# Gate, up and context weights turned by the host, and the four-chunk Hadamard mix moved from the weights to the inputs, in a two-layer gated kernel on one core

## The reference, cut to what matters

```
x = x + tanh(g_xattn[0]) * moe0(layernorm(x), tokens, ctx, ctx, ctx)      # expert by token id, 4 experts
x = x + tanh(g_ffn[0])   * hadamard_ffn(layernorm(x))
x = x + tanh(g_xattn[1]) * wkv(w, u, layernorm(x), ctx)                    # a scan over time, values = ctx
x = x + tanh(g_ffn[1])   * moe1(layernorm(x))                              # shared expert + top 2 of 8
```

```
g = silu(einsum('bsd,fd->bsf', h, Wg[e]));  u = einsum('bsd,fd->bsf', h, Wu[e])
y = einsum('bsf,df->bsd', g * u, Wd[e])
```

```
x      = fwht(x * SU_ug) / 64
x_up   = x @ W_up.T   * (Wscale_ug[:2048] * 64)
x_gate = x @ W_gate.T * (Wscale_ug[2048:] * 64)
x      = fwht(silu(x_gate) * x_up * SU_dp) / 64
x      = x @ W_down.T * (Wscale_dp * 64)
```

## Time and profile before

| | |
|---|---|
| median of 3 runs | 1342.69 us (1342.31 to 1342.88) |
| the profiled execution's own time | 1343.7 us |
| its span | 1342.0 us |
| instructions | 18348 |
| PE busy | 1256.9 us (94%) |
| DVE, ACT, POOL busy | 656.1, 446.4, 407.3 us |
| mean granted TensorE clock | 0.973 |

### The profile page before, as it was taken

How to read it: one execution, slowest core, us unless ns; L and a number is a source line. 1 busy time by engine, 2 the same in 40 slices (tenths; PEclk the granted TensorE clock), 3 DMA queues, 4 the chain that set the end, 5 groups by cost and what they waited for, 6 DMA issues and landing times.

```text
span 1342.0 us, 18348 instructions
## 1 busy us (share of the span) xinstructions
PE 1256.9 (94%) x6226; PEld 1062.6 (79%) x6227; DVE 656.1 (49%) x1104; ACT 446.4 (33%) x755; POOL 407.3 (30%) x333
## 2 busy tenths in 40 slices
PE   4999989999999999999999998999999999999960
PEld 3788878878888888888888877888788888888850
DVE  6555257544365655755456457766232232223216
ACT  3333342233234433343244346552222222222210
POOL 2221112000013211221234224247866240017854
PEclk9899999999999999999999999988999999999995
DMA  6822267553658875784866421045636242224457
GB/s 204 274 79 64 83 232 266 185 222 135 251 196 310 291 287 185 282 323 170 267 254 219 159 73 54 28 159 213 213 121 188 78 161 78 74 73 156 142 161 254
DMA packets 88395, 240.42 MB, mean 179 GB/s; under 512 B 8300, under 2 KB 35144, under 8 KB 76040
## 3 DMA queue, kind: packets, MB, share of 16 engines
q1 hardware_dynamic: 64824, 160.19, 33.1%
q0 software_dynamic: 23040, 79.08, 18.3%
q10 hardware_dynamic: 464, 0.27, 0.1%
HBM read 163.75 MB, written 75.76 MB: 178 GB/s over the span
## 4 chain that ended last, share of the span: by engine, by line
PE 87%; DVE 5%; DMA 2%; POOL 2%; issue 2%; ACT 1%; POOLq 0%; ACTq 0%; DVEq 0%
PE bank L1176 26%; PE bank L1346 19%; PE bank L1204 13%; PE bank L1384 10%; PE bank L1101 4%; PE bank L1121 4%; PE bank L1313 2%; PE bank L1131 2%; PE bank L1364 1%; POOL fin_low L784 1%; PE bank L1148 1%; DVE xres L1937 1%; DVE wl L1523 1%; PE bank L1087 1%; DMA yg<-y_sorted,slot 1%
## 5 line engine op out<-in xcount | busy, mean ns | idle before, releaser
L1176 PE MATMUL bank<-xTh,G 128*128 128x512 f32 x1024 | 278.6, 397 | 1.8 <-DVE xTl L1629 1.8
L1176 PEld LDWEIGHTS bank<-xTh,G 128*128 128x128 f32 x1024 | 188.8, 188 | 42.5 <-issue 3.4
L1346 PE MATMUL bank<-W,dxh 128*128 (+2 forms) x880 | 205.8, 376 | 8.4 <-DVE dmid L1783 5.1
L1346 PEld LDWEIGHTS bank<-W,dxh 128*128 128x128 f32 x880 | 164.2, 191 | 23.8 <-issue 8.5
L1204 PE MATMUL bank<-DN,bhh 128*128 128x512 f32 x512 | 158.0, 390 | 0.0
L1176 PE MATMUL bank<-xTl,G 128*128 128x512 f32 x512 | 137.4, 390 | 0.0
L1384 PE MATMUL bank<-W,dhh 112*128 (+1 forms) x440 | 126.1, 408 | 1.8 <-ACT dys L994 1.8
L1651 DVE SCALAR_TENSOR_TENSOR bs<-bank,tab,bs 128x512 f32<-128x512 f32 x64 | 47.5, 742 | 161.1 <-PE bank L1176 161.1
L1783 DVE TENSOR_TENSOR dmid<-bank,dsg 128x448 f32<-128x448 f32 x55 | 34.2, 622 | 173.9 <-ACT dsg L984 173.9
L1204 PEld LDWEIGHTS bank<-DN,bhh 128*128 128x128 f32 x512 | 96.2, 188 | 21.3 <-issue 1.7
L1176 PEld LDWEIGHTS bank<-xTl,G 128*128 128x128 f32 x512 | 96.1, 188 | 20.7
(11 more groups left out here) (250 smaller groups left out, 1989.6 us busy)
## 6 DMA issues: line engine op xcount, KB each, us to landing
G<-gate_up_split SPq DMA_DIRECT2D x48, 1024.0 KB, 7.0
DN<-down_split SPq DMA_DIRECT2D x24, 1024.0 KB, 4.9
wst<-in_L_ffn_w POOLq DMA_DIRECT2D x24, 896.0 KB, 5.9
gate_up_split<-G SPq DMA_DIRECT2D x16, 1024.0 KB, 7.3
y_all<-dys SPq DMA_DIRECT2D x55, 256.0 KB, 2.0
xs_sorted<-zero POOLq DMA_DIRECT2D x3, 3328.0 KB, 20.7
xsd<-xs_sorted SPq DMA_DIRECT2D x39, 256.0 KB, 3.0
down_split<-DN SPq DMA_DIRECT2D x8, 1024.0 KB, 3.9
```

The source lines that it names most:

```text
L1176: mm = pe.matmul(bank[m][:, :], G[:, c % 2, f, h, m, i, :], a[b % 2][:, i, :], start=(n == 0), stop=(n == 3 * DC - 1))
L1346: mm = pe.matmul(bank[o][:, 0:width], a[par][:, k, :], w[:, bass.ds(slot, 1), at + k * step:at + k * step + width].rearrange("p a n -> p ( ...
```

## The change

- The host hands over `ctx_2048` turned (`turned_context`) and the gate and up weights turned and blocked (`turned_weights`), so that each of them lies in memory as the products want it.
- `weights` on PE is gone: ACT and DVE split the context matrices straight from `nat` in SBUF. SP's load of the down weights waits for `s_wl` instead of `s_wT`.
- `prep_a` on PE is gone: `gu_high` and `gu_low` split straight from `wn` in SBUF. `load_wn` waits for `s_glo` instead of `s_pa`.
- The mix over the four chunks is now done on the inputs: `turn_high` writes float32 to `xq`, `turn_low` is gone, `half_mix` and `full_mix` on DVE make sums and differences (4 operations of 128 x 512 and 2 of 128 x 1024 for a batch). `mix` is now one float32 matmul of 128 x 512 in place of two float32r ones, and `Hr` is gone. `xq` lies where `xTl` lies, `xd` where `xTh` does.
- Since a mixed chunk needs all four turned ones, `mix` moves: of the next batch, chunks 0 and 1 in step 14, chunks 2 and 3 in step 15. In batch 0 the first two come after `up(14)`, in batches 1 and 2 ahead of it.
- `c_values` is gone: POOL loads the values turned (`vT`), DVE reads them from SBUF. `values(n + 1)` now waits for `sums(n)` (`s_cn`) and stands between `numerator` and `quotient`.

```diff
@@ engine SP
-            sp.wait_ge(s_wT, E0 * DC)
+            sp.wait_ge(s_wl, E0 * DC)
...
-                wait(sp, s_pa, 4 * (j - 1) + 2 * m + 2 if j else 0)
-                sp.dma_start(wn[m][:, :, :], wug_v[m][:, j * 8:j * 8 + 8, :]).then_inc(s_wn[m], 16)
+                wait(sp, s_glo, 4 * (j - 1) + 2 * m + 2 if j else 0)
+                sp.dma_start(wn[m][:, :, :], wug_v[m][j, :, :, :]).then_inc(s_wn[m], 16)
@@ engine POOL
-                    pool.wait_ge(s_cv, n)
+                    pool.wait_ge(s_cn, n)
                 c = n % DC
-                pool.dma_start(vnat[:, :, :], ctx_v[:, n // DC, :, c * P:(c + 1) * P]).then_inc(s_vn, 16)
+                pool.dma_start(vT[:, :], ctx_v[:, n // DC, c, :]).then_inc(s_vn, 16)
...
                     limit(n)
+                    numerator(n)
                     values(n + 1)
-                    finish(n)
+                    quotient(n)
@@ engine ACT
-                act.wait_ge(s_wT, j + 1)
-                act.activation(wh[:, j, :], bank[W_BANKS[j % 6]][:, :], ACT.Copy).then_inc(s_wh, 1)
+                act.wait_ge(s_ctx[j // DC], 16)
+                act.activation(wh[:, j, :], nat_at[j // DC][:, j % DC, :], ACT.Copy).then_inc(s_wh, 1)
...
-                act.mul(xTh[b % 2][:, c, :], bank[bk][:, :], tab[:, T_SUG + c:T_SUG + c + 1]).then_inc(s_bTh, 1)
+                act.mul(xq[b % 2][:, c, :], bank[bk][:, :], tab[:, T_SUG + c:T_SUG + c + 1]).then_inc(s_bTh, 1)
             def mixed_high(b, c, bk):
+                act.wait_ge(s_bq, 2 * b + 2)
...
-                    act.wait_ge(s_pa, 4 * j + 2 * m + i + 1)
+                    act.wait_ge(s_wn[m], 16 * (j + 1))
                     wait(act, s_kept[j % 2], 16 * 3 * (j // 2))
-                    act.activation(G[:, j % 2, i, 0, m, :, :], bank[banks[i]][:, :].rearrange("p (n c) -> p c n", c=DC),
-                                   ACT.Copy).then_inc(s_ghi, 1)
+                    act.activation(G[:, j % 2, i, 0, m, :, :], wn[m][:, DC * i:DC * i + DC, :], ACT.Copy).then_inc(s_ghi, 1)
@@ engine PE
-            def prep_a(j, m, banks):
-                pe.wait_ge(s_wn[m], 16 * (j + 1))
-                for i in range(2):
-                    for h in range(4):
-                        mm = pe.matmul(bank[banks[i]][:, h * P:(h + 1) * P], wn[m][:, 4 * i + h, :], cst[:, C_H4:C_H4 + P],
-                                       start=True, stop=True)
-                    mm.then_inc(s_pa, 1)
...
             def mix(b, c, bk):
-                pe.wait_ge(s_bTl, DC * b + c + 1)
-                pe.matmul(bank[bk][:, :], Hr[:, :], xTl[b % 2][:, c, :], start=True, stop=False)
-                pe.matmul(bank[bk][:, :], Hr[:, :], xTh[b % 2][:, c, :], start=False, stop=True).then_inc(s_hx, 1)
+                pe.wait_ge(s_bq, 2 * b + 1 + c // 2)
+                pe.matmul(bank[bk][:, :], cst[:, C_H:C_H + P], xq[b % 2][:, c, :], start=True, stop=True).then_inc(s_hx, 1)
...
-                if b + 1 < NB and b > 0 and step_at(k, 4) is not None:
-                    mix(b + 1, step_at(k, 4), 6)
+                if b == 0 and k == NK - 1:
+                    for c in range(2, 4):
+                        pe.wait_ge(s_hxl, DC + c - 1)
+                        mix(1, c, 4 + c)
+                if 0 < b < NB - 1 and k == NK - 2:
+                    mix(b + 1, 0, 6)
+                    mix(b + 1, 1, 7)
+                if 0 < b < NB - 1 and k == NK - 1:
+                    pe.wait_ge(s_hxl, DC * (b + 1) + 1)
+                    mix(b + 1, 2, 6)
+                    pe.wait_ge(s_co, n + DC)
+                    mix(b + 1, 3, 7)
                 up(g)
+                if b == 0 and k == NK - 2:
+                    pe.wait_ge(s_wdt, 2 * NJ)
+                    mix(1, 0, 6)
+                    mix(1, 1, 7)
@@ engine DVE
+            def half_mix(b, h):
+                t, s = xq[b % 2], xd[b % 2]
+                dve.wait_ge(s_bTh, DC * b + 2 * h + 2)
+                dve.tensor_tensor(s[:, 2 * h, :], t[:, 2 * h, :], t[:, 2 * h + 1, :], ALU.add)
+                chain(dve.tensor_tensor(s[:, 2 * h + 1, :], t[:, 2 * h, :], t[:, 2 * h + 1, :], ALU.subtract))
+            def full_mix(b):
+                t, s = xq[b % 2], xd[b % 2]
+                dve.tensor_tensor(t[:, 0:2, :], s[:, 0:2, :], s[:, 2:4, :], ALU.add).then_inc(s_bq, 1)
+                dve.tensor_tensor(t[:, 2:4, :], s[:, 0:2, :], s[:, 2:4, :], ALU.subtract).then_inc(s_bq, 1)
...
                 hidden_low(g)
+                if b < NB - 1 and k == (10 if b == 0 else 7):
+                    half_mix(b + 1, 0)
+                if b < NB - 1 and k == NK - 3:
+                    half_mix(b + 1, 1)
+                    full_mix(b + 1)
```

More of the change, by code:

```diff
@@ L944, in _ @@
                         turn_high(b + 1, step_at(k, 3), 6)
-                    if b + 1 < NB and step_at(k, 4) is not None:
-                        mixed_high(b + 1, step_at(k, 4), 6)
+                    if b + 1 < NB and k >= NK - 2:
+                        for c in range(2):
+                            mixed_high(b + 1, 2 * (k - NK + 2) + c, 6 + c)
                     if step_at(k, 3) is not None:
@@ L1710, in _ @@
                 norm(xnf[:, i, :], xres[:, i, :], i, rstd[:, i:i + 1]).then_inc(s_xnb, 1)
-            for c in range(DC):
-                turn_low(0, c, 2 + c)
+            half_mix(0, 0)
+            half_mix(0, 1)
+            full_mix(0)
             for f in range(2):
```

163 lines of the change are left out of this document (62 added, 101 removed).

## The result

The changed kernel takes 1325.1 us (median of 4 runs, 1323.46 to 1325.97); the kernel before, beside it, 1342.5 us. The ratio is 0.9864, 95% interval 0.9851 to 0.9877. That is 17.4 us less, where 20.7 were forecast, and inside the forecast's range of 1316.5 to 1327.0. The profiled execution took 1324.26 us, span 1322.6, so 19.4 less than the profiled one of before.

What follows compares the result with a forecast made beforehand. PE was taken to bound the kernel, busy 94% of the span and full in batch 0. The terms summed to -20.7 us, from 1343.7 to 1323.0, less 1.0 for the profiled execution: 1322.0 us median, range 1316.5 to 1327.0.

Steps and rivals of the forecast that it cites:

- `prep_a` in batch 0: Chunks 1 to 7 in batch 0: 14 removed groups of PE matmuls at 1.80 us each, -25.2 us.
- twelve `mix`: Batches 0 to 2: one float32 matmul at 0.87 us replaces two float32r at 0.46, each 0.41 dearer, +4.9 us.
- twelve `c_values`: Batches 1 to 3: removed value transposes save PE 0.45 us each, -5.4 us.
- step 14 of batches 1, 2: PE waits 1.3 us for DVE's first wide sum before mix, twice, +2.6 us.
- four `mix` ahead of step 0: Before the first gate: four float32 mix on the path delay it from 192.17 to 193.4 us, +1.3 us.
- clock ahead of step 0: Longer PE idling leaves the turn and some w16 at 1.2 GHz, +2.0 us, bounds 0 and 2.8.
- stage 1: PE's 64 transposes go, but the first tile waits for DVE; nothing gained, taken as 0.
- stage 4: Four removed value transposes bring 0 to 1.8 us, as PE partly waits for DVE; half taken, -0.9 us.
- the signs that the forecast named: Expected in the trace, among others: gate(0) about 3 us later, clock below 1 between 180 and 186 us.
- The first rival: Clock stays up ahead of step 0 and step 14's sums come in time: 1317.4 us, chance 0.21.
- The lock: Rival: DVE and POOL operations reading SBUF exclude each other; stage 4's scan loses up to 4.1 us, 1326.1 us, chance 0.12.
- the transfers: Rival: transfers bound batch 0, stores sinking to 170 GB/s, pairs of 26 us, 1375 us in all, chance 0.03.

Runs made afterwards that it cites:

- fill_turns: Changed kernel with two groups of eight unread 128 x 128 matmuls put back on PE in each of batch 0's first seven pairs of steps; 1358.03 us.
- fill_values: Changed kernel with four unread 128 x 128 transposes put back on PE at each of the sixteen places of the value transposes; 1336.71 us.
- norm_and_values: Changed kernel with early_norm's move, and the unread transposes put back where the value transposes stood in batches 1 and 2; 1333.94 us.
- early_norm: Changed kernel with DVE's normalisation for the next turned chunk moved ahead of the hidden product in batches 1 and 2; 1328.37 us.
- five: Changed kernel with early_norm, mix_first, last half mix and first full sum ahead of step 13's hidden product, batch 0's first half mix one step later; 1328.41 us.
- fill_stage1: Changed kernel with the 64 transposes ahead of stage 1 put back on PE, of a constant that nobody reads; 1333.31 us.
- three: Changed kernel with early_norm, mix_first, and the last half mix and whole full mix ahead of step 13's hidden product in batches 1 and 2; 1328.32 us.
- before_again: The kernel before, unchanged, profiled again on another chip; 1352.45 us.
- mix_first: Changed kernel with the four mix ahead of step 0 put before the two down-weight products, their low parts before the down scaling; 1332.77 us.

## Why the prediction was right, and where it was not

The sum of the changed parts, settled one by one (us; "measured" from the stretches and experiments above):

| term | forecast | measured |
|---|---|---|
| `prep_a` in batch 0 | -25.2 | -25.2 (pairs from 21.69 to 18.10) |
| twelve `mix` | +4.9 | +4.6 (0.49 gone, 0.87 come) |
| twelve `c_values` | -5.4 | -5.8 on PE, but 2.8 of it given back |
| step 14 of batches 1, 2 | +2.6 | +2.3 |
| turn of step 11, batch 0 | none | +0.65 |
| four `mix` ahead of step 0 | +1.3 | +1.24 |
| clock ahead of step 0 | +2.0 | 0 (some 0.6 in two other profiles) |
| stage 1 | 0 | -1.2 in the first profile, chance |
| stage 4 | -0.9 | +1.1 and +1.7 in two pairs, not clear of its spread |

*Right: `prep_a`.* The two `silu` starts a pair apart, which stand for the earlier trace rows:

```profile
200.74 0.69 ACT L863 ACTIVATE bs<-bank,tab 128x512 f32<-128x512 f32 x1 [0.27 <-PE bank L1152]
...
218.84 0.69 ACT L863 ACTIVATE bs<-bank,tab 128x512 f32<-128x512 f32 x1 [2.98 <-PE bank L1152]
```

18.10 us, where 18.4 had been said. That was 22.0 - 3.6, with 22.0 the mean of all seven pairs; the early ones take 18.1, those with a turn 18.5. The rule that made it right: PE was at 153.83 of 154 us, so what it sheds comes off the time one for one; fill_turns gives it back: 7 x 3.64 us.

*Right: `mix`, its wait in step 14, and its four ahead of step 0*. The wide sum took 1.22 us, 1.14 from start to start, where 1.15 was estimated; the idle stretches are 0.9 us in the profile and 1.1 from start to start, 1.3 forecast. (The forecast's own times give 1.2 in both places where it says +1.3: 488.8 - 487.6 and 193.4 - 192.17.)

*Wrong: "Twelve in batches 1 to 3: -5.4 us."* The step read the transposes' price from the earlier trace rows and took PE as full in all three batches, which the busy share says. It did not ask what PE would wait for next if it came sooner, though the forecast asked just that in step 14. In batches 1 and 2 PE was full, yet DVE's chain to the turn of step 3 already ended 0.27 us after PE, and those to the other three turns at most 0.2 us before it; 2.8 of 3.8 us went there. (The experiments give nearly the same by another way: put back, the transposes cost 1.1 us in these two batches, and 3.6 once the chain was shorter, 2.5 apart.) In batch 3, which has no turn, the whole 1.9 stayed. Two runs show it from both sides (fill_values, norm_and_values), one shows the way out (early_norm).

*Wrong: "the turn and some `w16` at 1.2 GHz ... I take +2.0 us".* The clock did fall, to 0.89 on average between 159.5 and 192 us, and 32 matmuls took 6.60 us. But they ended at 178.9, the norm had ended at 178.74, and the turn waited for the norm anyway, as its idle 1.10 us in the earlier trace rows had shown. The fault was to put a cost on the path without checking which of two waits ends last there. The turn itself ran at the full clock, which was back from 178.1 us on, so of the signs that the forecast named two did not show: the clock below 1 between 180 and 186 us, and `gate(0)` about 3 us later (192.20 instead of 192.17). The first rival left out this cost and the wait in step 14; half of it was right.

*Missed: the half mix of batch 0.* At step 10 it stands ahead of the normalisation on DVE, and the turn of step 11 came 0.65 us late; five, which moves it, gets that back.

*Not settled: "I take half, -0.9 us" in stage 4.* The stretch became longer by 1.66 and 1.14 us in the two pairs, less than it moves by itself. In the first profile 16 products at 836 us took 1.6 us longer than in the kernel before, and 0.7 us were waited for a load at 980 us. Whether the missing transposes have a part in it is open.

*The lock, and the transfers.* The lock struck a new operation of the scan just where the rival had said, but it cost DVE 1.3 us and PE nothing, and the kernel before had paid as much there. Where DVE and POOL did cost time, the rival had not looked: in the normalisation, which reads one tensor only and which the change does not touch. The forecast held against a lock that POOL's operations lie beside the reciprocal in batches 1 and 2; `limit` does not, and the 0.75 us that the normalisation loses beside it are more than PE waits at three of the four turns of a batch. The transfers reached 243 GB/s.

*Luck.* In the profiled pair the batches came out 2.5 us above the sum (2.8 given back and 0.65 missed, less 1.0 in which `mix`, the wait in step 14 and the values did better than priced), `gate(0)` 3.3 us below it (2.0 for the clock and 1.2 by chance), and what lies behind the batches 2.1 us above it. These partly cancelled: the profiled execution is off by 1.3 us, while the median lies 3.1 us above 1322.0, and 3.3 us of the 20.7 did not come.

## What to carry to other kernels

A full engine shows that its own work counts, not that taking work off it will pay: for every instruction taken away, find the next wait on that engine and how much earlier than its releaser the engine would then arrive. Here 0.48 us were saved four times a batch ahead of a turn. PE already came 0.3 us too early for the first and at most 0.2 us too late for the others, and 1.4 of 1.9 us were given back; moving DVE's normalisation into an idle stretch then brought 1.6 us a batch. When an operation on the chain that is waited for takes longer than the same one elsewhere (here 1.86 and 1.11 us), look for what runs beside it. And where an operation is moved on DVE, look at what POOL does at the new place, its issuing of transfers too, not only at the gap on DVE.

## What was not expected

The fall of the clock depends on more than the idle stretch before it. The changed kernel in stage 4, first a place where PE had been idle for 0.97 us:

```profile
835.17 1.03 PE L1327 MATMUL bank<-rtr,dxr 128*128 128x8 f32 x8 [0.97 <-issue]
836.05 0.63 PE L1283 MATMUL bank<-cst,xsd 128*128 128x128 f32 x4
836.44 2.97 PE L1316 MATMUL bank<-W,dxh 128*128 128x456 f32 x8
839.21 2.33 PE L1316 MATMUL bank<-W,dxl 128*128 128x456 f32 x8
```

Eight such products take 1.88 us at the full clock. In the kernel before the same place, with an idle 0.95 us, kept it (1.88 and 1.80). Of the fourteen profiles six lost it there (after, fill_stage1 with 3.26, fill_turns, three, five and norm_and_values) and eight kept it, all with 0.94 to 0.97 us idle. So a cost of 1.6 us comes and goes with an unchanged wait. The three profiles that have the value transposes at this place (before, before_again and fill_values) all kept it, those without them lost it in six of eleven; that is too few to say whether the transposes help. Stage 4 as a whole moved between 516.5 and 530.9 us from run to run of kernels that are alike there, in good part by waits that the profile books as "issue" (2.7 us in all in the changed kernel, 14.7 in mix_first, up to 8.3 in one place), which none of these runs explains.
